# Self-attention's softmax taken by rows, with the probabilities transposed on TensorE

## The reference, cut to what matters

```
x = x + cross_attention(layernorm(x), ctx)     # 1601 keys per batch
x = x + self_attention(layernorm(x))           # 64 keys per batch, causal
x = x + mixture_of_experts(layernorm(x))       # 8 experts, the two best of each token

# self_attention
q, k, v = heads of (x @ in_proj.T);  q = q / sqrt(16)
scores  = where(key <= query, q @ k.T, -inf)    # 64 x 64 for each batch and head
out     = softmax(scores, over the keys) @ v @ out_proj.T
```

## Time and profile before

| | |
|---|---|
| median of 3 runs | 688.7 us (686.59 to 689.65) |
| the profiled execution's own time | 688.74 us |
| its span, first to last instruction | 686.9 us |
| mean granted TensorE clock | 0.995 of full speed |
| PE, PEld busy | 658.6 us (96%), 540.8 us (79%) |
| DVE, ACT, POOL busy | 472.7, 326.5, 296.2 us (69%, 48%, 43%) |

### The profile page before, as it was taken

How to read it: one execution, slowest core, us unless ns; L and a number is a source line. 1 busy time by engine, 2 the same in 40 slices (tenths; PEclk the granted TensorE clock), 3 DMA queues, 4 the chain that set the end, 5 groups by cost and what they waited for, 6 DMA issues and landing times.

```text
span 686.9 us, 16172 instructions
## 1 busy us (share of the span) xinstructions
PE 658.6 (96%) x6611; PEld 540.8 (79%) x6619; DVE 472.7 (69%) x870; ACT 326.5 (48%) x532; POOL 296.2 (43%) x386
## 2 busy tenths in 40 slices
PE   6989999999999989999999999889999999999997
PEld 4668878878867867877887786666788999999996
DVE  3897757757667778674977857468678677666653
ACT  3355555554554554455446443446445444444431
POOL 1227798897676588675678766400000000000000
PEclk9999999999999999999999999989999999999999
DMA  5412110110000010011001000061103213320000
GB/s 157 149 26 72 26 50 25 40 36 25 27 25 26 26 49 26 26 30 46 9 20 48 1 2 1 2 247 54 70 1 124 79 46 124 122 100 22 0 0 31
DMA packets 12853, 34.12 MB, mean 50 GB/s; under 512 B 1515, under 2 KB 9972, under 8 KB 10612
## 3 DMA queue, kind: packets, MB, share of 16 engines
q1 hardware_dynamic: 12756, 33.19, 14.6%
q0 software_dynamic: 32, 0.01, 0.0%
HBM read 32.67 MB, written 0.52 MB: 48 GB/s over the span
## 4 chain that ended last, share of the span: by engine, by line
PE 81%; DVE 9%; issue 5%; ACT 2%; POOL 2%; DMA 0%; POOLq 0%; DVEq 0%; ACTq 0%
PE bank L1153 45%; PE bank L1339 13%; PE bank L1162 9%; PE bank L1223 5%; POOL prob_sum L481 2%; PE bank L1263 2%; PE bank L1272 2%; DVE prob_sum L481 1%; DVE ctx_lo L465 1%; DVE maxes L876 1%; ACT probs L718 1%; PE bank L1247 1%; PE bank L1184 1%; DVE shift L821 1%; DVE masked L811 1%
## 5 line engine op out<-in xcount | busy, mean ns | idle before, releaser
L481 POOL TENSOR_TENSOR prob_sum<-probs,prob_sum 128x256 f32<-128x256 f32 x336 | 266.4, 824 | 80.5 <-ACT probs L718 76.2
L718 ACT ACTIVATE probs<-bank 128x1024 f32<-128x1024 f32 (+1 forms) x104 | 106.6, 1025 | 125.6 <-PE bank L1339 110.6
L876 DVE TENSOR_REDUCE maxes<-bank 128x1 f32<-128x400 f32 (+1 forms) x256 | 131.3, 565 | 21.0 <-PE bank L1223 19.1
L700 ACT ACTIVATE h_raw<-bank,b_sb 128x512 f32<-128x512 f32 (+2 forms) x72 | 46.1, 641 | 106.5 <-PE bank L1153 106.3
L857 DVE SCALAR_TENSOR_TENSOR k_lo<-bank,bias_sb,k_hi 128x400 fp32r<-128x400 f32 (+2 forms) x64 | 40.4, 632 | 51.9 <-ACT k_hi L615 51.9
L1339 PE MATMUL bank<-qbd_hi,k_hi 64*128 64x256 f32 (+1 forms) x416 | 72.6, 343 | 1.0 <-ACT probs L718 0.6
L1153 PE MATMUL bank<-w_hi,h_hi 128*128 128x256 f32 x256 | 72.6, 284 | 0.0
L1153 PE MATMUL bank<-w_hi,h_lo 128*128 128x256 f32 x256 | 72.1, 282 | 0.0
L1153 PE MATMUL bank<-w_lo,h_hi 128*128 128x256 f32 x256 | 72.0, 281 | 0.0
L1162 PE MATMUL bank<-probs,v_sb 128*32 128x128 f32 (+1 forms) x1664 | 67.9, 281 | 2.5 <-DVE masked L811 2.0
L1153 PE MATMUL bank<-wv_hi,ctx_hi 128*128 128x256 f32 (+1 forms) x208 | 65.8, 316 | 2.4 <-DVE maxes L876 2.0
(11 more groups left out here) (156 smaller groups left out, 1430.8 us busy)
## 6 DMA issues: line engine op xcount, KB each, us to landing
raw<-in_w SPq DMA_DIRECT2D x16, 1024.0 KB, 6.8
ctx_raw<-in_ctx_t SPq DMA_DIRECT2D x16, 400.0 KB, 3.6
ctx_raw<-in_ctx_t SPq DMA_DIRECT2D x8, 402.0 KB, 3.7
ctx_raw<-in_ctx_t SPq DMA_DIRECT2D x8, 399.0 KB, 3.6
w_sb<-in_w_t SPq DMA_DIRECT2D x1, 1280.0 KB
w_raw<-in_w_t SPq DMA_DIRECT2D x2, 256.0 KB, 4.6
result<-x_all SPq DMA_DIRECT2D x1, 512.0 KB, 3.0
x_all<-in_x SPq DMA_DIRECT2D x1, 384.0 KB, 4.0
```

Source lines behind the costliest of these rows:

```text
L481: ins = engine.tensor_tensor(prob_sum[0:ROWS[k], cols], probs[0:ROWS[k], s % 2, cols], acc[0:ROWS[k]], ALU.add)
L700: nc.scalar.activation(h_raw[:, c % 2, 0:width], bank[:, at, 0:width], ACT.Gelu, bias=b1_sb[:, bass.ds(e, 1), c:c + 1].rearrange("p a b -> ...
L718: nc.scalar.activation(probs[0:ROWS[k], s % 2, :].rearrange("p (g n) -> p g n", g=G), bank[0:ROWS[k], score_bank(b, k):score_bank(b, k) + ...
L876: nc.vector.tensor_reduce(maxes[:, g * PAIRS + j, c:c + 1], src[:, 0:width], AX.X, ALU.max).then_inc(read_dve, 1)
```

## The change

The first scores' layout is kept. The mask and the row maxima are made as before, into a new tile `soft` that holds both batches; VectorE subtracts the maxima there (`subtract_maxima`), ScalarE takes the exponential of all 128 partitions x 512 at once (`own_exponentials`, one step later), VectorE sums the rows, takes the reciprocal and multiplies (`divide_rows`, one more step later). TensorE then turns `soft` over: units `t00`..`t11`, four instructions each, true transposes for the first batch and matmuls with the identity for the second, whose results are on partitions 64 to 127. ScalarE copies them to `probs2` (four copies of 64 x 512). `o` loses its denominators, and VectorE's part after it is two instructions on half the columns (`own_values`). The second batch's spread queries are written one step after `s0`.

```diff
-CHAIN_AT = {3: ["y1"], 5: ["xt1"], 6: ["qk", "v"], 8: ["s0"], 10: ["st00", "st01"], 12: ["s1"], 13: ["st10", "st11"],
-            15: ["o0"], 16: ["o1"], 18: ["y2"], 20: ["xt2"], 21: ["router"], 24: ["gt"], 25: ["b2"]}
-CHAIN_AT_LAST = {2: ["y1"], 4: ["xt1"], 5: ["qk", "v"], 7: ["s0"], 8: ["st00", "st01"], 10: ["s1"],
-                 11: ["st10", "st11"], 12: ["o0", "o1"], 14: ["y2"], 16: ["xt2"], 17: ["router"], 19: ["gt"],
-                 20: ["b2"]}
-CHAIN_ALONE = {1: ["y1"], 2: ["xt1"], 3: ["qk"], 5: ["s0", "s1", "v"], 6: ["st00", "st01"], 7: ["st10", "st11"],
+CHAIN_AT = {3: ["y1"], 5: ["xt1"], 6: ["qk", "v"], 8: ["s0"], 10: ["s1"], 11: ["t00", "t01"], 13: ["t10", "t11"],
+            14: ["o0"], 15: ["o1"], 17: ["y2"], 19: ["xt2"], 20: ["router"], 24: ["gt"], 25: ["b2"]}
+CHAIN_AT_LAST = {2: ["y1"], 4: ["xt1"], 5: ["qk", "v"], 7: ["s0"], 9: ["s1"], 10: ["t00", "t01"], 12: ["t10", "t11"],
+                 13: ["o0", "o1"], 15: ["y2"], 17: ["xt2"], 18: ["router"], 21: ["gt"], 22: ["b2"]}
+CHAIN_ALONE = {1: ["y1"], 2: ["xt1"], 3: ["qk"], 5: ["s0", "s1", "v"], 7: ["t00", "t01", "t10", "t11"],
                8: ["o0", "o1"], 9: ["y2"], 11: ["xt2"], 12: ["router"], 15: ["gt"], 16: ["b2"]}
-FIRST_HIDDEN = {0: [0, 1], 1: [2], 3: [3, 4], 9: [5, 6], 11: [7]}
-FIRST_SPLIT_H = {0: [0, 1], 2: [2], 6: [3], 7: [4], 10: [5], 11: [6], 12: [7]}
-FIRST_OUTPUT = {1: [0], 2: [1], 8: [2, 3, 4], 11: [5], 12: [6, 7]}
+FIRST_HIDDEN = {0: [0, 1], 1: [2], 3: [3, 4], 6: [5], 7: [6], 9: [7]}
+FIRST_GELU = {0: [0, 1], 1: [2], 3: [3, 4], 8: [5, 6], 9: [7]}
+FIRST_SPLIT_H = {0: [0, 1], 2: [2], 4: [3], 7: [4], 8: [5], 11: [6], 12: [7]}
+FIRST_OUTPUT = {1: [0], 2: [1], 6: [2, 3], 8: [4], 9: [5], 12: [6, 7]}
...
 ScalarE
+            def own_exponentials(units, s, t):        # after the units of step s
+                for kind in units.chain.get(s - 1, []):
+                    if kind in ("s0", "s1"):
+                        bi = int(kind[1])
+                        act.wait_ge(soft_ready, 2 * t + bi + 1)
+                        nc.scalar.activation(soft[:, bi], soft[:, bi], ACT.Exp).then_inc(soft_exp_done, 1)
...
 VectorE
+            def subtract_maxima(bi):
+                link(nc.vector.tensor_reduce(neg_max2[:, bi], soft[:, bi], AX.X, ALU.max, negate=True))
+                nc.vector.tensor_tensor(soft[:, bi], soft[:, bi], by_row(neg_max2[:, bi]), ALU.add).then_inc(soft_ready, 1)
+            def divide_rows(bi, count):
+                dve.wait_ge(soft_exp_done, count)
+                link(nc.vector.tensor_reduce(row_sums2[:, bi], soft[:, bi], AX.X, ALU.add))
+                link(nc.vector.reciprocal(row_sums2[:, bi], row_sums2[:, bi]))
+                nc.vector.tensor_tensor(soft[:, bi], soft[:, bi], by_row(row_sums2[:, bi]), ALU.mult).then_inc(rows2_ready, 1)
...
-                if "st01" in before and units is not TAIL:
-                    units.wait_read_act(dve, read_act, "st01")
+                if "s0" in before and units is not TAIL:
                     spread_own_queries(1, qbd2)
+                for kind in units.chain.get(s - 2, []):
+                    if kind in ("s0", "s1"):
+                        divide_rows(int(kind[1]), 2 * t + int(kind[1]) + 1)
...
 TensorE
+                    pe.wait_ge(rows2_ready, 2 * t + bi + 1)
+                    for j in range(PAIRS):
+                        turned, own_rows = dst[bi * Q:bi * Q + Q, j * P:j * P + P], soft[:, bi, g * PAIRS + j, :]
+                        if bi == 0:
+                            ins = nc.tensor.transpose(turned, own_rows, ident[:, :])
+                        else:
+                            ins = nc.tensor.matmul(turned, own_rows, ident[:, :], start=True, stop=True)
```

More of the change, by code:

```diff
@@ L124, in both_tiles @@
     return [("M", ROW_TILES * u + r) for u in pairs for r in range(ROW_TILES)]
-READ_BY_ACT = {"p1", "p2", "p3", "v", "V", "VL", "X", "xt1", "qk", "st00", "st01", "st10", "st11", "xt2", "router", "gt"}
+READ_BY_ACT = {"p1", "p2", "p3", "v", "V", "VL", "X", "xt1", "qk", "t00", "t01", "t10", "t11", "xt2", "router", "gt"}
 class Units:
@@ L172, in wait_read_act, with wait_read_dve @@
         eng.wait_ge(by_act, self.before[1] + self.counts(n + 1)[1])
+    def wait_read_dve(self, eng, by_dve, kind):
+        n = next(n for s in range(STEPS) for n, k, _ in self.at[s] if k == kind)
+        eng.wait_ge(by_dve, self.before[2] + self.counts(n + 1)[2])
     def wait_shift(self, eng, by_act, bi):
@@ L291, in perceiver_kernel @@
         unused = sb("unused", [P, 1])
-        warm = sb("warm", [P, 1])
+        warm = sb("warm", [P, 4])
         mask_sb = sb("mask_sb", [P, HG + 2])
@@ L657, in step @@
                         unit(units, n, kind, u, t, b, parity)
+                own_exponentials(units, s, t)
             def prepare(k):
@@ L805, in normalize, with own_values, by_row @@
                                         ALU.mult).then_inc(done, 1)
+            def own_values(src, bi, read):
+                both = src[:, 0:G * P].rearrange("p (g s q) -> p g s q", g=G, s=2)
+                part = odd2[:, bi]
+                link(nc.vector.tensor_scalar(part, both[:, :, 1, :], mask_sb[:, HG + 1:HG + 2], None, ALU.mult))
+                nc.vector.scalar_tensor_tensor(out=o2_t[:, :, bi * Q:bi * Q + Q], in0=both[:, :, 0, :],
+                                               scalar=mask_sb[:, HG:HG + 1], in1=part, op0=ALU.mult, op1=ALU.add).then_inc(read, 1)
+            def by_row(values):
+                return values.unsqueeze(2).broadcast_to([P, G * PAIRS, Q])
+            def subtract_maxima(bi):
[6 more added lines that the diff above has]
+                nc.vector.tensor_tensor(soft[:, bi], soft[:, bi], by_row(row_sums2[:, bi]), ALU.mult).then_inc(rows2_ready, 1)
             def own_heads(src, read, count):
@@ L889, in unit @@
                     bi = int(kind[1])
-                    own_heads(src, read_dve, units.before[2] + units.counts(n + 1)[2])
-                    divide_heads(o2_t[:, :, bi * Q:bi * Q + Q], o2_ready)
+                    own_values(src, bi, read_dve)
                 elif kind == "b2":
@@ L910, in after_units @@
                     elif kind in ("s0", "s1"):
-                        link(nc.vector.tensor_reduce(neg_max2[:, :], masked[:, :, :], AX.X, ALU.max, negate=True))
-                        on_diagonal((shift2_alone if units is TAIL and kind == "s1" else shift2)[:, :, :],
-                                    neg_max2[:, :], shift2_ready)
+                        subtract_maxima(int(kind[1]))
             def route(units, t):
@@ L1020, in tile @@
                     b = 2 * t + bi
+                    if k == 1 and not is_first(b):
+                        dve.wait_ge(denom_done, b)
+                        at = (bi + 1) % 2 * Q
+                        own_heads(bank[:, O, :], o_read, b)
                     if more == bi == 1:
@@ L1029, in tile @@
                         spread_queries(b + 1, (bi + 1) % 2)
-                    if k == 1 and not is_first(b):
-                        dve.wait_ge(denom_done, b)
-                        at = (bi + 1) % 2 * Q
-                        own_heads(bank[:, O, :], o_read, b)
                     if k == FIND_SHIFT_AT and more > bi:
@@ L1103, in _ @@
                     split_h(c, c, DONE_TILES * P, c >= 4)
-                if s == SECOND_LO_AT:
-                    for j in range(PIECES):
-                        split_w(1, 2 * PIECES + j, j)
+                if s in SECOND_LO_AT:
+                    split_w(1, 2 * PIECES + SECOND_LO_AT[s], SECOND_LO_AT[s])
             def last_rows():
```

64 lines of the change are left out of this document (27 added, 37 removed).

## The result

| | before | changed |
|---|---|---|
| median | 689.8 us (20 runs beside it) | 686.97 us (20 runs) |
| ratio, 95% interval | | 0.9968 (0.9953 to 0.9983) |
| span of the profiled execution | 686.9 us | 684.9 us |
| mean granted clock in it | 0.995 | 0.982 |

What follows compares the result with a forecast made beforehand. TensorE was taken to bound the kernel, busy 96% of the span. Gains of 2.2 us (two middle tiles), 3.1 (last tile) and 2.6 (fourth tile's chain) sum to 7.9, from 688.7 to 680.8 us; range 672 to 687.

Steps and rivals of the forecast that it cites:

- The fourth tile's chain: Fourth tile: 3.67 us less matmul work, less 0.7 for late transposes and 0.4 for ScalarE's copy; gain 2.6 us, bounds 1.5 to 3.7.
- The middle tiles' waits: First half of each middle tile: waits at s1 and t00 plus ScalarE's added work, charged 3.6 us, bounds nothing to 5.5.
- TensorE's work: Each of four self-attention tiles: 6.32 us of work removed, 2.65 added, net 3.67 us less, 14.7 over four.
- Shift wait: Second half of each middle tile: earlier gates remove a 1.55 us wait for the shift; 1.0 us gain taken.
- The wait at `s1`: Middle tiles, step 10: TensorE waits 1.1 us for the second batch's queries, which VectorE spreads late.
- the wait at `t00`: Middle tiles, first batch's transposes: TensorE waits 2.0 us for VectorE's division, queued behind the second batch's mask, maxima and subtraction.
- rival (c): VectorE becomes the bound as operations beside GpSimd's sums stretch by half and the clock falls; 691.8 us, chance 0.06.
- rival (b): Clock falls in the middle tiles: two 3.3 us half-speed stretches after t00's waits cost 1.7 us each; 684.2 us, chance 0.19.
- Last tile: Tile t = 3: 3.0 us gained by step 13, less 0.9 for y2, plus 1.0 of gate wait; 3.1 us, bounds 1.5 to 5.
- "Even" for the bank of `o0`: Last tile, step 14: own_heads before the sum frees the bank 1.22 us earlier, offset by two own_values of 0.7 each.
- Rival (a): TensorE's whole saving arrives because VectorE is ahead at s1 and t00; 18 us less, 670.7 us, chance 0.17.
- Rival (d): Transposes cost the skill's price, or the last tile's waits eat its gain; 686 us, no change, chance 0.06.

Runs made afterwards that it cites:

- e10: Changed kernel with middle tiles' s1, transposes, outputs one step later, last tile's transposes and outputs too, fourth chain's seventh-chunk split earlier but its output still step 12; 671.37 us.
- e1: Changed kernel with s1, both batches' transposes and both outputs one step later in the middle tiles; 677.79 us, ratio 0.9829 to the kernel before.
- e12: Changed kernel with seven eighths of GpSimd's sums of probabilities left out in the middle tiles, serving for durations alone; 681.83 us.
- e4: Changed kernel with the seventh chunk's split in the fourth tile's chain in step 9 instead of 11, its output in step 11 instead of 12; 692.46 us.
- e5: Changed kernel with only the last tile's table changed: first batch's transposes in step 11 instead of 10, both outputs in 14 instead of 13; 685.70 us.
- e13: Changed kernel with overwritten matmuls added in the fourth tile's chain, four ahead of xt2's wait and two ahead of the router's; 685.94 us.
- e8: Changed kernel with VectorE dividing the first batch's probabilities before masking the second batch's scores in the middle tiles, TensorE's order untouched; 684.52 us.
- e11: e10 with overwritten matmuls added in the fourth tile's chain, four ahead of xt2's wait and two ahead of the router's; 668.35 us.
- e2: Changed kernel with s1 moved behind the first batch's transposes in the middle tiles, second batch's transposes and outputs one step later; 691.72 us.
- e9: Changed kernel with the first batch's eight transposes written as matmuls against the identity, same order; 700.18 us, ratio 1.0176 to the kernel before.
- e3: Changed kernel with overwritten matmuls added in the middle tiles, three ahead of s1's wait and four ahead of t00's; 694.50 us.

## Why the prediction was right and wrong

The sum failed in two steps. The fourth tile's chain was forecast at +2.6 us, with one small wait, chunks that "fill the rest" and no fall of the clock: it measured -1.97, by 2.1 us more of waits and 2.4 of clock. The middle tiles' waits were charged 3.6 us a tile, with VectorE's operations at 0.69, 1.34 and 0.97 us and the clock at nothing: they measured 4.4 and 5.3 in one profile, and 7.3 and 5.4 in three others. That the median fell inside the range, by 0.03 us, is luck.

- **TensorE's work, 3.67 us a tile: right.** PE's busy time fell by 9.9 us although five half-speed stretches stand in it against two; in e10, which has one, it fell by 16.2. e1's middle tiles gain 4.9 and 4.8, as 3.67 with the shift term gives. The eight transposes took 1.03 to 1.06 us (taken: 0.9), the identity form 1.96 with its end (taken: 1.75). The Trainium skill's 275 ns ("TensorE: Matmul & The Clock Gate", Part 4) is the length of one transpose's record here, 272 to 276 ns on average; one behind the other they cost 0.13 us each, so the smaller price that I took was the right one.
- **Shift wait: right.** 3.1 to 0.7 us in two tiles, 1.2 each where I took 1.0; the last tile's gate wait (1.4, foretold as 1 to 1.5) too.
- **The wait at `s1`, 1.1 us: too small in t = 1** (1.6; 0.9 in t = 2), and **the wait at `t00`, 2.0 us: too small** (3.2 wherever TensorE came at full speed). I took the subtraction at the mask's 0.69, and the spread and the split at their durations in the earlier trace rows, 1.34 and 0.97. From the first maxima to the product 1.7 us are the difference (1.09 and 1.16 for 0.69, 1.63 for 1.34, 1.51 for 0.97), and e12 takes it away. Two things were wrong in it. The mask and the maxima, which I set against rival (c), don't have two SBUF inputs, so their 0.68 and 0.69 said nothing of the subtraction. And the earlier trace rows's spread and split had stood beside GpSimd's sums already (190.43 and 193.40, before's GpSimd row):

```profile
188.34 14.23 POOL L481 TENSOR_TENSOR prob_sum<-probs,prob_sum 128x256 f32<-128x256 f32 x16 [0.85 <-ACT probs L718]
```

  So GpSimd beside it does not always stretch an operation, and one row doesn't tell what the next place will cost. I had the stretch as rival (c) with 0.06 and a threshold too far off to count: a contention that does not make VectorE the bound still lengthens each wait.
- **The clock: forecast left it out, rival (b) had it, in part of the places.** Rival (b) priced 3.3 us stretches in the middle tiles. In t = 2 one came, in t = 1 the stretch stood behind `s1` and was mostly hidden, since VectorE was late for `t00` anyway: its wait is 1.27 behind the slow stretch and 3.2 without one. In e4, e5 and e13 it stands at `t00`, 7 us long, and tile t = 1 is 2.9 us worse. What (b) did not have is the fourth chain.
- **Fourth tile's chain, +2.6: the worst step, -1.97.** I forecast one small wait (0.4) and that expert chunks "fill the rest". TensorE's waits between the last exponential and the gates went from 2.7 to 4.9 us (denominators 0.7 to 1.4, transposes 0.5, `xn` 0.5 to 0.8, the router 0.6, `h_lo` 0.6), because the chunks were now used up before the router: before, fifteen matmuls of them stood between `xt2` and it (from 508.8 to 511.0 us), now none does. The clock took 2.4 more (e13). With the clock up the chain is 0.4 to 0.5 us better than before, no more.
- **Last tile, 3.1: right by size, not by terms.** "Even" for the bank of `o0` and 1.4 for `t00` should have been 2.07 and 1.85, and a stretch of 7 us at half speed followed; that these made up for each other with the other terms is luck. e5 without these gains 8.9 us in that tile.
- **Rival (a), 670.7:** e10 took 671.37. Its middle tiles gain 5.0 and 4.8 us, as (a) has them (4.9): the saving was there, and the tables gave it away. The rest of the agreement is luck: last tile 8.9 against 4.5, fourth chain -0.1 against 3.7.
- **Rival (d), 686:** it has the measured number, but not the cause: eight transposes cost 1.05 us and not 2.2, and the last tile kept 2.55 of its 3.1.

How much the clock took over many executions can be estimated. 54 spans of before (those beside the experiments) carry 5.2 us of lost clock on average, 20 of the changed kernel 10.7. Within e8's ten spans 1 us of lost clock goes with 0.88 us of time, within e5's ten 0.82, within the changed kernel's twenty 0.71, within before's 54 0.72, within e13's twelve 1.05. At 0.7 to 1.05 the 5.6 us between them are 4 to 6 us of the 5.7 missing from the forecast, and what is left, 0 to 2, would be the longer waits themselves. That two things vary together doesn't show that one makes the other, and a changed kernel without lost clock was never seen (its clocks are 0.974 to 0.988), so this split is an estimate.

Open: what sets the length of a half-speed stretch, when GpSimd beside it stretches an operation of VectorE, and where the 3 us between the medians of e10 and e11 come from. A change of e1's kind with the division also put first was not tried.

## What to carry to other kernels

When work leaves the bounding engine, price every new handover twice: the wait itself, with the longest duration on record of each operation of the feeding engine that has the same kind of inputs and the same neighbours, and the half-speed stretch that may come with it. Then give the consumer one step of distance before timing anything: here one step in two tiles was worth 9 us, more than three times what the whole change had brought. And list the mean clock of every execution beside its time: that is where part of the gain was hidden here.

## What the runs showed that I had not expected

- Waits at `t00` of 3.2 us or more went with a granted clock of 0.50 in 11 of 11 cases (profiles of the changed kernel, e2, e4, e5, e9, e13), and in 7 of them it had fallen before the wait was over. The last tile's wait of 2.07 us for the bank of `o0`, with one of 0.4 to 0.7 us close behind, was followed by it in 9 of 9, the 1.85 us wait at `t00` of that tile in 3 of 9, the 1.6 us wait at `s1` in 1 of 6, the two of 0.53 us at `t00` in e8 in neither. It is not a matter of the wait alone.
- At the same three waits in the fourth chain (0.8, 0.6, 0.6 to 0.8 us) the stretch lasted 3 us in e1 and e2, 7 in the changed kernel, e5 and e9, and 24 in e3, e8 and e12.
- A half-speed stretch ahead of a late engine cost nothing that shows: t = 1 gained 0.5 us with it (changed kernel) and 0.15 without (e3). One at the wait itself did: -2.4 us (e4, e5, e13).
- An f32 operation of two SBUF inputs over 128x512 takes VectorE 0.69 us alone and up to 1.17 beside GpSimd's sums; the spread over 128x1024 1.23 and up to 1.77; the diagonal 1.23 and 1.54. Not every one is stretched: of the spreads that stood wholly beside the sums (all kernels but e12) 39 took 1.21 to 1.25 us and 39 took 1.34 to 1.77. Row sums, maxima and a mask read from PSUM stay at 0.67 to 0.69 in both.
